# On-chip buffers placed at multiples of 64 bytes instead of 32

## The reference

```
nx = layer_norm(x); q = nx @ Wq; k = ctx @ Wk; v = ctx @ Wv
evidence = softmax(q k^T / sqrt(256)) @ v
combined = concat(nx, evidence, cond)                  # 768 wide
probs = softmax(combined @ router_W + router_b)        # 3 experts
h = silu(combined @ e_w1 + e_b1)                       # 3 x 512 wide
routed = sum_e probs_e * (h_e @ e_w2 + e_b2)
gate = sigmoid(silu(combined @ gate_w1 + b) @ gate_w2 + b)
x = x + gate * (routed @ out_w + out_b)
# second block: 16 heads of width 16
xq, xkv = ada_ln(x, cond), ada_ln(ctx, cond)
x = x + softmax(q16 k16^T / 4) v16 @ Wp + bp
```

## Time and profile before

| | |
|---|---|
| median of 3 runs | 438.74 us (lowest 438.71, highest 1439.61) |
| span of the profiled execution, first to last instruction | 436.9 us |
| busy share of the span: PE, PEld | 97%, 88% |
| DVE, ACT, POOL | 68%, 51%, 40% |
| chain that ended last: PE, DVE, ACT | 77%, 15%, 3% |
| mean granted TensorE clock | 0.996 |

### The profile page before, as it was taken

The page is one execution under the profiler, slowest core; times in us unless marked ns, Lnnn a source line. Parts: engine busy times, 40 slices in busy tenths (PEclk is TensorE's granted clock), DMA queues, the critical chain, the costliest instruction groups (busy, mean ns, idle before and its releaser), DMA issues.

```text
span 436.9 us, 9623 instructions
## 1 busy us (share of the span) xinstructions
PE 422.1 (97%) x3629; PEld 384.7 (88%) x3629; DVE 296.3 (68%) x748; ACT 223.6 (51%) x487; POOL 175.0 (40%) x184
## 2 busy tenths in 40 slices
PE   7899999999999999999999999999999899979996
PEld 6578999989998899889998899889988898868876
DVE  2785566674675696739863797389658755891797
ACT  2868643255347543764367246724672356326271
POOL 4545474553353526324523344344433632330020
PEclk9999999999999999999999999999999999998999
DMA  8786102531100210023000300030003021300301
GB/s 288 252 298 269 50 2 47 142 91 31 44 5 1 63 59 30 24 78 116 2 5 13 109 1 5 14 86 0 5 20 80 0 56 28 80 3 26 72 3 48
DMA packets 16837, 27.80 MB, mean 64 GB/s; under 512 B 3800, under 2 KB 9112, under 8 KB 16664
## 3 DMA queue, kind: packets, MB, share of 16 engines
q1 hardware_dynamic: 16664, 27.19, 21.2%
q10 hardware_dynamic: 128, 0.01, 0.0%
HBM read 15.94 MB, written 2.10 MB: 41 GB/s over the span
## 4 chain that ended last, share of the span: by engine, by line
PE 77%; DVE 15%; issue 3%; ACT 3%; DMA 1%; SPq 1%; ACTq 0%
PE hidden_banks L1688 7%; PE hidden_banks L1690 7%; PE hidden_banks L1689 7%; PE score_banks L1695 6%; PE score_banks L2060 5%; PE token_bank L1688 5%; PE token_bank L1689 5%; PE token_bank L1690 5%; PE score_banks L2030 4%; PE value_bank L2083 3%; PE value_bank L2086 3%; PE value_bank L1695 3%; DVE head_maxima L1463 3%; PE hidden_banks L1913 2%; DVE sums L1477 2%
## 5 line engine op out<-in xcount | busy, mean ns | idle before, releaser
L1620 POOL TENSOR_TENSOR hidden_low<-hidden,hidden_high 128x512 fp32r<-128x512 f32 x56 | 72.8, 1300 | 123.5 <-ACT hidden_high L1072 123.4
L1463 DVE TENSOR_REDUCE head_maxima<-score_banks 128x2 f32<-128x308 f32 x128 | 54.6, 473 | 17.1 <-PE score_banks L2030 15.0
L1688 PE MATMUL hidden_banks<-normed_high,hidden_w_high 128*128 128x256 f32 x224 | 64.2, 287 | 0.8 <-issue 0.8
L1689 PE MATMUL hidden_banks<-normed_high,hidden_w_low 128*128 128x256 f32 x224 | 62.5, 279 | 0.0
L1690 PE MATMUL hidden_banks<-normed_low,hidden_w_high 128*128 128x256 f32 x224 | 62.5, 279 | 0.0
L1132 ACT ACTIVATE exp_ring<-score_banks 128x512 f32<-128x512 f32 x96 | 52.6, 600 | 18.8 <-PE score_banks L2060 17.5
L1072 ACT CAST hidden_high<-hidden 128x512 fp32r<-128x512 f32 x56 | 34.8, 622 | 48.2 <-DVE hidden L1380 48.1
L1688 PE MATMUL token_bank<-expert_out_high,hidden_high 128*128 128x256 f32 x192 | 55.7, 290 | 0.0
L1064 ACT ACTIVATE hidden<-hidden_banks 128x512 f32<-128x512 f32 x56 | 33.3, 595 | 41.6 <-PE hidden_banks L1913 40.0
L1690 PE MATMUL token_bank<-expert_out_low,hidden_high 128*128 128x256 f32 x192 | 53.4, 278 | 0.0
L1689 PE MATMUL token_bank<-expert_out_high,hidden_low 128*128 128x256 f32 x192 | 53.4, 278 | 0.0
(11 more groups left out here) (294 smaller groups left out, 1111.5 us busy)
## 6 DMA issues: line engine op xcount, KB each, us to landing
unit_weights<-units SPq DMA_DIRECT2D x7, 768.0 KB, 6.0
query_stack<-queries_high SPq DMA_DIRECT2D x56, 64.0 KB, 2.0
tokens<-x SPq DMA_DIRECT2D x8, 256.0 KB, 3.7
query_stack<-queries_low SPq DMA_DIRECT2D x28, 64.0 KB, 2.0
w_slice<-units SPq DMA_DIRECT2D x7, 256.0 KB, 3.0
out<-tokens SPq DMA_DIRECT2D x7, 256.0 KB, 2.4
w_T<-folds SPq DMA_DIRECT2D x6, 256.0 KB, 6.1
pair_keys<-keys_high SPq DMA_DIRECT2D x16, 77.0 KB
```

What stands on the lines that cost most here:

```text
L1463: v.tensor_reduce(MX[:, s, first:first + step + 1:step], S[:, ring_of[key][0], 0:2 * CTX].rearrange("p (j n) -> p j n", j=2), AX.X, ALU.ma ...
L1620: nc.gpsimd.tensor_tensor(SL[:, ring(t, u), :], TB[:, ring(t, u), :], raw(SH[:, ring(t, u), :]), ALU.subtract).then_inc(gpsimd_h, 1)
L1688: mm(out_, lh, rh, start=start, stop=False, skip_group_check=skip)
L1689: mm(out_, ll, rh, start=False, stop=False, skip_group_check=skip)
```

## The change

Both places that round a size now round to 64. No instruction, no wait and no order on any engine differs; only byte offsets do.

```diff
--- before.py
+++ after.py
@@ -472,7 +472,7 @@
                 size *= n
             o = at[0] if offset is None else offset
             if offset is None:
-                at[0] += (size + 31) // 32 * 32
+                at[0] += (size + 63) // 64 * 64
             return nc.alloc_sbuf_tensor_at(name, shape, dt, offset=o)
 
         def run(start, parts):
@@ -483,7 +483,7 @@
                 size = 4
                 for n in shape[1:]:
                     size *= n
-                start += (size + 31) // 32 * 32
+                start += (size + 63) // 64 * 64
             return made + [start]
```

## The result

The changed kernel takes 440.45 us (median of 11 runs, 439.04 to 442.30) against 439.02 us (11 runs), a ratio of 1.0041 with a 95% interval of 1.0025 to 1.0057. By the ratio that is 1.8 us slower (the two medians as they stand are 1.4 us apart). It is inside 2%, but it is clear of noise, and the time lies just outside the range of 437.0 to 440.4 us.

The account below looks back on a forecast made before the run. The prediction took PE, through its matmuls, to bound the kernel. Its terms for matmuls, the other engines and DMA were 0 + 0 + 0, leaving the median at 438.7 us, with a range of 437.0 to 440.4 us.

Parts of the forecast that it names:

- What bounds the kernel: Whole kernel: PE bounds it, busy 422.1 of 436.9 us; time is matmul count by pace, plus some 15 us of gaps.
- Matmul, moving operand: Matmuls on lines 1688 to 1690: the moving operand's position does nothing visible to durations; cost taken 0.
- My bound of 1 ns on 3,629 matmuls: All matmuls: medians of like groups differ by 1 ns, so at most 3.6 us either way.
- Third rival: Main matmul groups, both operands coming to 64 past 128: 10 ns on 1,696 matmuls, 17 us slower; chance 0.02.
- the sign that the prediction names for being wrong: Matmul groups in the changed profile: a median duration that moves by 3 ns or more.
- Matmul, weights: Weight loads on PE, 188 ns beside a matmul: position costs 0, within the 3.6 us bound.
- DVE, ACT, POOL: Instructions of these three engines: position costs 0; bound 0.8 us either way for DVE and ACT, POOL hidden behind PE.
- DMA: Copies and loads: position costs 0; the bound for a gain is 0.5 us.
- first rival: Copies into `query_stack`: eight waits each 0.06 us shorter, 0.5 us in all, giving 438.2 us; chance 0.12.
- Second rival: One long copy wait or clock fall more or less: 1.6 us either way, 437.1 or 440.3 us; chance 0.12.

Follow-up runs that it names:

- e1: The kernel before with every buffer moved 32 bytes further, so all starts are multiples of 64 and operands stay 64 apart: 438.19 us, ratio 0.9984.
- e5: The kernel before with 32 bytes left free ahead of the tokens, so operands are 32 or 96 apart within 128: 441.09 us, ratio 1.0044.
- e3: The changed kernel with 64 bytes left free ahead of the tokens, weights at 64 past a multiple of 128, tokens at 0: 438.28 us, ratio 0.9974.
- m1: Matmuls alone, the reference's computation left out, rows of 12 for pairs of operand starts in steps of 32 bytes: 113 to 121 ns a matmul.
- m2: Matmuls alone, moving operand 0 to 960 bytes beyond the weights, shuffled and reversed order: 114 to 118 ns at 64 within 128.
- e4: The kernel before with 384 bytes left free ahead of the normed values, moving operand 192 beyond the weights within 512: 438.01 us, ratio 0.9976.

## Why the prediction was wrong

**What bounds the kernel.** Right: PE, and its time is the number of matmuls by the pace of one. But I then read durations, not the pace, although I had named the pace.

**Matmul, moving operand: the step that failed.** "The spread with four positions, 8 ns, is no wider than the spread with one, 10 ns. So position does nothing that I can see, and the cost taken is 0." Measured are 1.9 ns a matmul. The comparison could not show it, for three reasons. It looked at each operand's own position, and e1 shows that this indeed does nothing; what counts is the distance between the moving operand and the next weights. The keys' matmuls go through all distances, so their median is a mixture. And a spread of 10 ns was taken as the limit of what can be seen, where 2 ns on 1,776 matmuls are enough. A row of the kernel before that gives a hint was not used: line 2129 fills a gap with matmuls whose moving operand and weights are the same buffer, at distance 0, and where they run back to back they go at 119.5 ns, beside 117 ns in the main groups. My bound of 1 ns on 3,629 matmuls, 3.6 us, did take in the result, and I then cut the range inside it.

**Third rival: the right mechanism, mis-sized.** It named the groups and the places (32 and 96 before, both at 64 after). The term was 10 ns on 1,696 matmuls, 17 us. Measured are 1.2 ns, 1.8 ns and 3.2 ns in the three groups, in all 0.8 + 0.8 + 1.8 = 3.4 us on those 1,696 (line 1913 taken to lose as much as the group that it belongs to), and half of it comes through. I had tied its price to a spread and its chance, 0.02, to the mixed rows of the keys; at its real price it was no case of "slower by 2%" but the likeliest case within 2%. Its condition was also too narrow: e5 shows that 32 and 96 apart cost as much as lying alike. For `expert_out_*` and `hidden_*` it had weights and moving operand the wrong way round, which changes nothing in the distance of 64. And the sign that the prediction names for being wrong, a median duration that moves by 3 ns or more, would have misled: on `hidden_w_low` it moved by 2 ns for the loss, and stayed at 281 ns when e3 took the loss back.

**Matmul, weights.** 0 is right for the loads themselves: they stay at 188 ns in both kernels. Their effect is on the matmul beside them.

**DVE, ACT, POOL.** Right. Line 1318 at 373 ns against 376, busy times within 0.5 us, and e3 is not slower with all starts at multiples of 64.

**DMA and the first rival.** Copies land in 2.0 us as before, so the rival gave nothing. By the rule of the Trainium skill's page "DMA: Bandwidth & Descriptors", section "How a descriptor splits into AXI transactions", the estimate was 7% of the data part, under 0.03 us on a landing of 2.0; these landings can't tell it. The waits for `queries_high` did get shorter, by 1.3 us, but with landings unchanged this fits PE coming later.

**Second rival.** The size, 1.6 us for the fall of the clock, is what the runs give (441.54 against 439.97 us). But it is no case of its own: a lower mean clock comes in about half of the runs of one kernel and belongs to the spread on both sides. It does mislead a comparison of two single profiles: the changed kernel was 2.1 us behind at 380 us and 0.7 us at 400 us.

## What to carry to other kernels

Rounding buffers to a larger power of two is not neutral and not by itself good: it can bring two streams that are read at the same time into a worse place to each other. In a kernel bound by fp32r matmuls with 256 columns, look at where the moving operand begins against the next weights within 128 bytes, and keep them 64 apart; a gap of 64 bytes ahead of one group of buffers is enough. It makes the fast pace of 113 ns possible and does not ensure it. To see such an effect, take the distance between starts of back to back matmuls, group by group, since a nanosecond or two is below the scatter of durations and still moves a kernel of thousands of matmuls.

## What the runs showed of the hardware

- PE's pace depends on how its two reads lie to each other. With fp32r, 256 columns and 128 wide weights, the pace at full clock was 114 to 118 ns with the moving operand 64 bytes (within 128) from the next weights, and 118 to 120 ns at 0 and 96. At 32 it was 116.5 to 119.5 ns in matmuls alone and 118.6 ns in the kernel. In bf16 it was 109 ns and in fp32 216 ns at each of the four distances tried.
- At a distance of 64 there are two speeds, 113.3 and 117.8 ns, and the same pair of buffers ran at either (m1, m2). The share of each in a kernel's groups goes with their mean pace.
- A part of the pattern stays open: what chooses between the two speeds, and so why `token_bank` became 0.9 ns slower in e4 without a change of its own operands, and the other order with 512 columns. That the cause is a shared part of the memory was not tested beyond the pace; the runs show the dependence, not the circuit.
- The changed kernel went at 439.97 us where the mean clock was 1.000 and at 441.54 us where it was 0.991 to 0.992, in about half of the runs each.
